# A graph network layer pair on one core: edge weights of the second layer read from PSUM, and TensorE waiting quarter by quarter

## The reference

```python
x = _layernorm(x + _L0_gnn_ref(x, ..., src, dst, edge_type_5, node_type_3), axis=-1)
x = _layernorm(x + _L1_gnn_ref(x, edge_weight1, ..., src, dst, edge_type_16), axis=-1)

# second layer
all_msg = jnp.einsum('nf,rfo->rno', h, weight)            # 16 relations
msg = all_msg[rel_type, src] * norm                       # norm: one weight per edge
all_gate = jnp.einsum('nf,rf->rn', h, gate_weight[..., 0])
gate = jax.nn.sigmoid(all_gate[rel_type, src])[:, None]
msg = msg * gate
agg = jax.ops.segment_sum(msg, dst, num_segments=n_nodes)
return jax.nn.relu(agg)
```

## Time and profile before

| | us |
|---|---|
| median of 3 runs | 1767.35 |
| the profiled execution | 1766.86 |
| its span | 1765.1 |
| PE busy | 1235.6 |
| DVE busy | 1126.1 |
| POOL busy | 941.0 |
| second layer, first gather's start | 1169.9 |
| second layer, last gather's start | 1741.1 |
| mean granted TensorE clock | 0.831 |

### The profile page before, as it was taken

One profiled execution on the slowest core, in us unless ns is written; L12 is line 12 of the kernel. 1 busy time (PEld: TensorE's weight loads), 2 busy tenths in 40 slices (PEclk: granted clock), 3 DMA queues, 4 the chain that ended last, 5 costly groups with the idle time before them and its releaser, 6 DMA issues.

```text
span 1765.1 us, 20638 instructions
## 1 busy us (share of the span) xinstructions
PE 1235.6 (70%) x6342; PEld 1023.8 (58%) x6342; DVE 1126.1 (64%) x1759; ACT 607.8 (34%) x1199; POOL 941.0 (53%) x905
## 2 busy tenths in 40 slices
PE   5799999558999999999999999943333333333333
PEld 4688888547878787878787888732222222222221
DVE  4733446378777777777777778426666666666663
ACT  3222222314454545454545454522222121222221
POOL 1042000277565655555555564037777777777773
PEclk9899999869999999999999999975555555556555
DMA  6354446567676767777777776343333333333332
GB/s 145 121 145 135 132 133 226 179 181 216 209 233 214 235 213 227 221 229 219 224 228 221 233 211 220 85 122 105 107 105 105 107 106 107 106 108 105 106 109 58
DMA packets 103849, 286.53 MB, mean 162 GB/s; under 512 B 20805, under 2 KB 40409, under 8 KB 100661
## 3 DMA queue, kind: packets, MB, share of 16 engines
q0 software_dynamic: 56032, 169.34, 32.1%
q1 hardware_dynamic: 47774, 116.71, 21.8%
HBM read 189.33 MB, written 96.65 MB: 162 GB/s over the span
## 4 chain that ended last, share of the span: by engine, by line
PE 49%; POOL 26%; issue 12%; DMA 5%; DVE 5%; ACT 1%; SPq 1%; DVEq 0%; ACTq 0%; POOLq 0%
POOL kv L680 25%; PE banks L866 12%; PE banks L894 11%; PE banks L824 5%; PE banks L758 5%; PE banks L842 4%; DMA kv_table<-tstage 3%; PE banks L812 3%; PE banks L780 2%; PE banks L766 2%; PE banks L786 1%; POOL kv L666 1%; PE banks L834 1%; PE banks L858 1%; DMA x_all<-in_x 1%
## 5 line engine op out<-in xcount | busy, mean ns | idle before, releaser
L666 POOL DMA_INDIRECT kv<-kv_table,rows x416 | 457.9, 1101 | 295.9 <-PE banks L894 126.2
L680 POOL DMA_INDIRECT kv<-message_table,rows x416 | 445.8, 1072 | 202.2 <-issue 126.4
L983 PE MATMUL banks<-wr_r,onehot_r 128*121 128x512 f32 x416 | 193.3, 641 | 395.6 <-DVE wr_r L1585 395.6
L983 PEld LDWEIGHTS banks<-wr_r,onehot_r 128*121 128x121 f32 x416 | 125.0, 316 | 463.6 <-DVE wr_r L1585 313.0
L866 PE MATMUL banks<-wr_r,x1T_r 128*121 128x512 f32 x1248 | 323.2, 402 | 2.2 <-ACT mstage L1128 2.2
L1219 ACT ACTIVATE wr_r<-banks 128x1024 fp32r<-128x1024 f32 x104 | 106.4, 1023 | 416.6 <-DVE banks L1593 416.6
L866 PEld LDWEIGHTS banks<-wr_r,x1T_r 128*121 128x121 f32 x1248 | 216.7, 183 | 51.4 <-ACT mstage L1128 3.3
L1128 ACT ACTIVATE mstage<-banks,gate 121x256 f32<-121x256 f32 x416 | 171.1, 471 | 152.2 <-PE banks L866 134.5
L894 PE MATMUL banks<-kv,onehot_r 128*121 128x264 f32 x832 | 202.9, 393 | 0.0
L1593 DVE TENSOR_TENSOR banks<-kv,norms 128x1024 f32<-128x1024 f32 x104 | 128.0, 1230 | 91.4 <-DMA kv<-message_table,rows 91.4
L1585 DVE TENSOR_TENSOR wr_r<-banks,wr_r 128x1024 fp32r<-128x1024 f32 x104 | 127.2, 1223 | 86.1 <-ACT wr_r L1219 86.1
(11 more groups left out here) (141 smaller groups left out, 1490.5 us busy)
## 6 DMA issues: line engine op xcount, KB each, us to landing
message_table<-mstage SPq DMA_DIRECT2D x104, 484.0 KB
kv_table<-tstage SPq DMA_DIRECT2D x26, 1210.0 KB
kv<-kv_table,rows POOLq DMA_INDIRECT x416, 5.4
kv<-message_table,rows POOLq DMA_INDIRECT x416, 2.8
query_table<-qstage_r SPq DMA_DIRECT2D x26, 242.0 KB
qb_r<-query_table SPq DMA_DIRECT2D x26, 242.0 KB
kv<-in_Wr POOLq DMA_DIRECT2D x2, 2048.0 KB, 14.3
xb<-in_x SPq DMA_DIRECT2D x26, 121.0 KB
```

Of the source, the lines that this page charges most:

```text
L666: pool.indirect_dma_start(kv[:, n % 2, u, 0:2 * C], None, ktab, bass.IndirectOffsetOnAxis(ap=rows[:, 0, n, u:u + 1], axis=0)).then_inc(kv_ ...
L680: pool.indirect_dma_start(mrows[:, r.q, u, :], None, mtab, bass.IndirectOffsetOnAxis(ap=rows[:, 1, r.number, u:u + 1], axis=0)).then_inc(l ...
L983: last = mm(b_l[r.q][:NODES, 0:2 * C], onehot_r[:, r.par, u, :], rows_r[:, r.par, u, :, :].rearrange("p k c -> p (k c)"), start=(u == 0), ...
```

## The change

Two things change, both in the second layer. First, `norms` (26 x 16 floats in each partition) is copied once into PSUM bank 3, and `weigh_rows` reads its weights from there, as `b_norms`; the wait behind the copies counts one more. Second, TensorE waits for `l_low` before each of the four quarters of a round, for that quarter alone, where it had waited twice, for two quarters each time.

```diff
--- before.py
+++ after.py
@@ -320,6 +320,7 @@
         b_gate = bank[5][:NODES, 0:RT]
         b_l = (bank[0], bank[1], bank[0], bank[1])
         b_iota = bank[2][:, 0:NODES]
+        b_norms = bank[3][:, 0:ROUNDS * U].rearrange("p (j u) -> p j u", j=ROUNDS)
         b_weighed = [pairs[2 + k][:, :, :].rearrange("p b (u c) -> p (b u) c", u=2) for k in range(2)]
         b_qe, b_ohT, b_agg, b_tmp, b_out, b_m = bank[0:2], bank[2], bank[3], bank[4], bank[5], bank[6:8]
 
@@ -978,8 +979,8 @@
                     pe.wait_ge(l_z, r.two_back)
                 pe.wait_ge(l_oh, r.done)
                 for u in range(U):
-                    if u % (2 * GU) == 0:
-                        pe.wait_ge(l_low, r.parts(u // GU + 1))
+                    if u % GU == 0:
+                        pe.wait_ge(l_low, r.parts(u // GU))
                     last = mm(b_l[r.q][:NODES, 0:2 * C], onehot_r[:, r.par, u, :],
                               rows_r[:, r.par, u, :, :].rearrange("p k c -> p (k c)"),
                               start=(u == 0), stop=(u == U - 1))
@@ -1589,7 +1590,7 @@
 
                 dve.wait_ge(l_landed[r.q][g], r.used)
                 u = slice(g * GU, g * GU + GU)
-                w = norms[:, bass.ds(r.number, 1), u].rearrange("p j u -> p (j u)").unsqueeze(2).broadcast_to([P, GU, C])
+                w = b_norms[:, bass.ds(r.number, 1), u].rearrange("p j u -> p (j u)").unsqueeze(2).broadcast_to([P, GU, C])
                 v.tensor_tensor(b_weighed[g % 2], mrows[:, r.q, u, :], w, ALU.mult).then_inc(l_weighed, 1)
 
             def l1(r):
@@ -1608,7 +1609,8 @@
             dve.wait_ge(agg_done, ROUNDS * G)
             dve.wait_ge(ends_kept, ROUNDS)
             v.tensor_copy(b_iota, iota_n[:, :]).then_inc(const_ready, 1)
-            dve.wait_ge(const_ready, 2)
+            v.tensor_copy(b_norms, norms[:, :, :]).then_inc(const_ready, 1)
+            dve.wait_ge(const_ready, 3)
             mark(Turn(dve, 0, 2))
             turns(dve, l1)
             finish(Turn(dve, QUADS, LB - 1))
```

## The result

The changed kernel takes 1717.3 us (median of 4 runs, 1713.59 to 1721.28) against 1767.59 for the kernel before: a ratio of 0.9713, 95% interval 0.9686 to 0.974. The forecast was 1714.2.

A forecast was written before the change was run, and what follows sets the result against it. GpSimd's gathers (line 680) bound the second layer. Holds 52.3, less remainder 1.0, plus tail 1.9, gave 53.2 us off the 1765.1 span: 1711.9, with 1.8 around the span and 0.5 to the median 1714.2 us, range 1708 to 1728.

The forecast's parts named there:

- the 52.3 us: Second layer's gathers: excess over their median time, in 98 long gathers at the multiply of line 1593; all expected gone.
- held point: Point 0.13 us after a gather's start where it seems to be held until VectorE's instruction is done.
- One SBUF input does not hold: VectorE instructions with at most one SBUF input were said not to lengthen gathers; those with two contend.
- The remainder at line 1560, +1.0: Line 1559 before, two SBUF inputs, 0.42 us a round: may just touch gathers; +1.0 us, bounds nothing and 11.
- The multiply keeps 1.23 us: Line 1593's multiply, then reading and writing PSUM, was taken to cost 1.23 us, like its nearest rows.
- The rival of two passes: Multiply reading and writing PSUM takes 2.30 us, making VectorE the bound: 1796 us; chance 5%.
- The copy costs nothing: Copying 416 elements once takes some 0.6 us, covered by VectorE's 11.39 us wait for the first landing.
- VectorE's shortest round is 18.9, 1.1 us of slack: VectorE's round without landing waits, 18.9 us, lies 1.1 under GpSimd's 20.0, so gathers stay the bound.
- The tail, -1.9: After the last subtraction, half of the last eight matmuls (3.77 us) can run earlier: -1.9 us, bounds 0 and 3.8.
- TensorE's quarters are worth nothing in the rounds: Quarter waits gain nil in rounds: with eight matmuls the end is 0.5 us late, inside 1.1 us of slack.
- the ring: Not in the prediction: last subtraction, eight matmuls, low sum, closing work, first subtraction, one-hot, three more quarters; 20.7 us.
- The rival "VectorE becomes the bound, mildly": Bank reads, loop branches or closer spacing add 1.5 to 3 us to VectorE's round: 1724 to 1763 us; chance 9%.

The follow-up runs named there:

- e2: Changed kernel with TensorE waiting twice a round again, so the weights in PSUM alone: 1725.78 us, ratio 0.9763.
- e4: Changed kernel with the one-hot comparison reading its iota row from SBUF in place of PSUM: 1746.82 us, ratio 0.9884.
- e8: Kernel before, with each multiply of 1024 elements cut into two of 512: 1746.33 us, ratio 0.9882.
- e5: Weights in PSUM and two TensorE waits a round, with VectorE's closing work moved behind the one-hot matrix: 1717.65 us, ratio 0.9712.
- e7: Changed kernel plus a whole further one-hot comparison on VectorE each round, result thrown away: 1734.57 us, ratio 0.9821.
- e6: Changed kernel plus half a one-hot comparison more on VectorE each round, result thrown away: 1712.95 us, ratio 0.969.
- e1: Changed kernel again, without an edit: 1715.47 us, ratio 0.9708.
- e10: Changed kernel once more without an edit, on the same chip as two later runs: 1715.38 us, ratio 0.9715.
- e3: Kernel before with TensorE's quarter waits alone, weights still in SBUF: 1769.81 us, ratio 1.0011.

## Why the prediction was right, and where it was not

- *GpSimd is the bound and the 52.3 us are holds of line 1593.* Shown by e2, which takes the hold away with the weights alone (first to last gather 518.9 us), and by e4 and e8, which bring it back or shorten it. All of it went at the multiply and 1.5 came back at line 1560, which leaves 51.0.
- *Which gathers are held.* The prediction counts gathers whose held point lies inside an instruction. That is not enough: a gather that started first is not held, whatever the operands. So not all of its 55 gathers at line 1418 and 103 at line 1585 speak for the case; those that started behind the instruction do, 36 and 67 of them, and none is long.
- *One SBUF input does not hold.* This is true of the instructions counted there, but not of every instruction. Line 1571 (`tensor_scalar`: `z` from SBUF, and two columns with one number per partition) held a gather by 0.10 us in e5 and one by 0.12 us in e7. The sum does not hang on it.
- *The remainder at line 1560, +1.0.* 1.5, 1.2 and 1.2 us in three profiles. The working from the earlier trace rows puts its start 0.27 us ahead of a gather's (1.25 - 0.98); it is 0.13 to 0.42 ahead in 25 of the 26 rounds.
- *The multiply keeps 1.23 us.* It takes 1223 ns. The rival of two passes falls.
- *The copy costs nothing.* It takes 0.58 us, and VectorE's first wait for a landing is 10.81 us in place of 11.39. The second layer starts in the same window of times with it and without it.
- *VectorE's shortest round is 18.9, 1.1 us of slack.* Shown by e6 and e7: 21.0 - 2.16 = 18.8.
- *The tail, -1.9.* -1.7. Half of the eight was not half of the time: four take 2.06, and two such bursts 0.35 us more than one of eight (2 x 2.06 - 3.77).
- *TensorE's quarters are worth nothing in the rounds.* This step failed: with the weights in PSUM they are worth 8 to 9 us there (e2 against e1: 10.3 by the medians, 9.9 by the profiles from the first gather on, each less the 1.7 of the tail). The working had put the low sum 0.5 us late once, "inside the 1.1 us of slack". But that slack is time between VectorE's last quarter and the next landing, and the late low sum comes after the landing, in the first quarter. The lateness pushes the round's remaining quarters, so also its last subtraction, and the next low sum is later still. The rounds of e2 show it grow: from first to second multiply 8.6, 9.0, 9.4, 10.2 us in successive rounds, then mostly 10.2 to 10.4, where the ring itself is the bound (8.4 to 8.5 in e1). I had compared only each engine's own work with GpSimd's round, and not the ring that passes through three engines.
- *The rival "VectorE becomes the bound, mildly".* It had a chance of 9% and the right size for e2 (1724 to 1763; e2 has 1725.8), but the ring through TensorE is not among the causes that it names.
- *The sum.* It came out near since both edits were in the kernel: the second kept the first one's gain. That is luck. By the same working the weights alone would give 1714.2 + 1.9 = 1716.1 us, and they give 1725.8. Forecast for the changed kernel's part from first gather on: 595.2 - 53.2 = 542.0; measured 542.6 in its profile and 542.2 in e1 and e10. The 3.1 us between forecast and the first median are within what runs of one kernel differ.

## What to carry to other kernels

Where VectorE and GpSimd's gathers run side by side, look at the operands of every VectorE instruction: with two in SBUF it holds a gather that starts in it until it ends. A small second operand can be moved to a free PSUM bank; where there is none, shorter instructions hold for less (e8, 20.7 us faster with the weights left in SBUF). They cost time here since GpSimd is the bound: in the first layer of the kernel before 81 gathers of line 666 are held too, by 64.6 us in all, but the chain has only 1% of the span there. Before such a gain is booked, walk every ring that comes back to the same instruction one round later, across engines, and compare its length with the new bound; slack of one engine does not cover it. And an edit that gives nothing alone (e3) can be what lets another keep its gain.

## What the runs showed of the hardware that was not expected

*Who starts first decides.* In the kernel before, a multiply that starts with a gather does not hold it:

```profile
1429.46 1.27 DVE L1593 TENSOR_TENSOR banks<-kv,norms 128x1024 f32<-128x1024 f32 x1
1429.46 0.95 POOL L680 DMA_INDIRECT kv<-message_table,rows  x1 [0.30 <-issue]
```

The gather takes its 0.95 us, and here the multiply is the longer one, 1.27 us in place of 1.22. A gather that starts 0.03 us behind a multiply (1539.32) takes 2.00 us. Line 1560 shows the same: in e5 and e6, where nearly all of its instructions start after a gather, it covers the held point of 12 and of 8 gathers and holds none. The first layer of the kernel before has both sides as well: of the gathers that start behind a VectorE instruction and have their held point in it, all 29 at line 1509 and all 26 at line 1410 (two SBUF inputs each) are long, and none of 36 at line 1418 (one).

*A hold with one input tensor in SBUF*, in e5:

```profile
1388.62 0.41 DVE L1571 TENSOR_SCALAR x<-z,mv,rstd 121x256 f32<-121x256 f32 x1
1388.79 1.05 POOL L681 DMA_INDIRECT kv<-message_table,rows  x1 [0.30 <-issue]
```

1389.03 + 0.81 = 1389.84 is the gather's end again. No run was made to find out when such an instruction holds a gather.

*TensorE's clock.* The granted clock is the share of full speed; in these rows it stands behind the busy times (stretch, PE, PEld, DVE, ACT, POOL, clock, DMA share, GB/s), kernel before and changed kernel:

```profile
1200.00:1740.00 540.00, 179.74 (x388) 116.56 (x389) 335.02 (x370) 115.60 (x148) 420.89 (x392) 0.57 0.37 106
```

```profile
1200.00:1690.00 490.00, 200.35 (x390) 109.27 (x389) 331.14 (x369) 115.14 (x149) 371.04 (x391) 0.50 0.41 117
```

With bursts of four matmuls the clock stays at its lower level, 0.50, which is 1.2 GHz, though as many matmuls are done in a shorter stretch. With bursts of eight it rises for moments (0.57). Over 1200 to 1690 us the other runs agree: 0.50 in e1, e3 and e10 with four, 0.52, 0.57 and 0.58 in e2, e5 and e8 with eight. In e2 some bursts of eight take 2.93 to 3.07 us in place of 3.77 (the second one below has a clock of 0.67 over 1343 to 1347 us), and the round of such a burst is 19.8 to 19.9 us and not 20.7:

```profile
1336.59 3.77 PE L984 MATMUL banks<-wr_r,onehot_r 128*121 128x512 f32 x8 [10.05 <-DVE wr_r L1586]
1343.48 3.00 PE L984 MATMUL banks<-wr_r,onehot_r 128*121 128x512 f32 x8 [3.13 <-DVE wr_r L1586]
```

What the lower clock costs with quarter waits was not measured by itself; in the rounds TensorE is not the bound.
